# A quantised feed-forward stage: its loop written out, and its integers transposed by DMA

## What is computed

```python
def act_quant(x):
    scale = 127.0 / jnp.clip(jnp.max(jnp.abs(x), axis=-1, keepdims=True), 1e-05)
    return jnp.clip(jnp.round(x * scale), -128, 127) / scale
def bit_linear(x, w):          # w is quantised to -1, 0, 1 times a scale
    return jnp.einsum('bsd,hd->bsh', act_quant(x), weight_quant(w))
h = bit_linear(layernorm(x), w1)                  # 128 -> 512
h = depthwise_conv1d(h, conv_w, conv_b)           # three taps along the sequence
h = silu(h)
x = x + tanh(g_ffn[1]) * bit_linear(h, w2)        # 512 -> 128
```

## Time and profile before

| | |
|---|---|
| median of 3 runs | 987.94 us (987.78 to 988.53) |
| profiled execution | 991.65 us, its span 989.9 us |
| busy in the span: PE, PEld | 947.1 us (96%), 739.9 us (75%) |
| DVE, ACT, POOL | 833.3 us (84%), 748.9 us (76%), 588.4 us (59%) |
| quantised stage | from about 803 us to the end |
| DMA over the span | 21.49 MB, mean 22 GB/s |

### The profile page before, as it was taken

How to read it: one execution, slowest core, us unless ns; L and a number is a source line. 1 busy time by engine, 2 the same in 40 slices (tenths; PEclk the granted TensorE clock), 3 DMA queues, 4 the chain that set the end, 5 groups by cost and what they waited for, 6 DMA issues and landing times.

```text
span 989.9 us, 36747 instructions
## 1 busy us (share of the span) xinstructions
PE 947.1 (96%) x11854; PEld 739.9 (75%) x11854; DVE 833.3 (84%) x2349; ACT 748.9 (76%) x1709; POOL 588.4 (59%) x1232
## 2 busy tenths in 40 slices
PE   6999999999989999999899999999999899999997
PEld 4777777777779999998877677676777667777775
DVE  7888888889978888888887888888887778889886
ACT  5878787787787777766656777777777878888885
POOL 5545454544536555656885544545454378888884
PEclk9999999999999999999998999999999999999999
DMA  3501011100000000000000000000000000000001
GB/s 110 178 24 43 25 38 32 32 22 11 13 2 1 0 0 0 0 0 0 2 12 24 13 12 21 11 21 11 21 11 1 2 10 22 23 22 21 24 21 31
DMA packets 19361, 21.49 MB, mean 22 GB/s; under 512 B 3553, under 2 KB 12001, under 8 KB 19297
## 3 DMA queue, kind: packets, MB, share of 16 engines
q1 hardware_dynamic: 19296, 20.68, 6.9%
HBM read 16.48 MB, written 4.19 MB: 21 GB/s over the span
## 4 chain that ended last, share of the span: by engine, by line
PE 39%; issue 5%; POOL 4%; DVE 2%; ACT 2%; DVEq 0%; POOLq 0%; ACTq 0%
PE bank L1295 9%; PE bank L1318 7%; PE score L1372 4%; PE score L1579 2%; PE score L1581 2%; PE bank L1438 2%; PE score L1580 2%; PE score L1364 2%; PE bank L1342 2%; PE bank L1334 1%; PE bank L1330 1%; PE bank L1337 1%; ACT prob_t L599 1%; PE bank L1604 1%; POOL xdq L573 1%
## 5 line engine op out<-in xcount | busy, mean ns | idle before, releaser
L599 ACT ACTIVATE prob_t<-bank 128x512 f32<-128x512 f32 x256 | 152.8, 597 | 122.1 <-PE bank L1295 114.0
L952 DVE TENSOR_REDUCE smax<-score 128x16 f32<-128x1024 f32 x128 | 156.8, 1225 | 46.0 <-PE score L1372 30.2
L1295 PE MATMUL bank<-const,prob 128*128 128x128 f32 x1024 | 165.9, 285 | 14.1 <-ACT prob_t L599 14.1
L594 ACT ACTIVATE prob<-prob 128x512 f32<-128x512 f32 x256 | 161.2, 630 | 8.9 <-DVE prob L961 8.2
L1318 PEld LDWEIGHTS bank<-vb,prob_t 128*64 128x64 f32 x4096 | 130.4, 138 | 49.4 <-issue 42.9
L961 DVE TENSOR_TENSOR prob<-score,smax 128x512 f32<-128x512 f32 x256 | 165.0, 686 | 1.3
L1295 PEld LDWEIGHTS bank<-const,prob 128*128 128x128 f32 x1024 | 108.0, 141 | 67.6 <-issue 58.6
L1318 PE MATMUL bank<-vb,prob_t 128*64 128x18 f32 x4096 | 143.2, 213 | 0.0
L411 POOL TENSOR_SCALAR kj<-k_sb,const 128x512 f32<-128x512 f32 x124 | 85.5, 696 | 73.7 <-issue 38.5
L674 ACT ACTIVATE eb_t<-eb,gwt 128x128 f32<-128x128 f32 x256 | 81.4, 391 | 41.7 <-POOL eb_acc L452 24.7
L382 POOL TENSOR_TENSOR a_ve<-a_mv,const 128x4 f32<-128x4 f32 x32 | 6.5, 203 | 153.3 <-DVE a_mv L954 145.7
(11 more groups left out here) (162 smaller groups left out, 2334.6 us busy)
## 6 DMA issues: line engine op xcount, KB each, us to landing
ctx_t<-in_ctx SPq DMA_DIRECT2D x32, 256.0 KB, 2.7
x_all<-in_x SPq DMA_DIRECT2D x16, 256.0 KB, 2.8
out_x<-x_all SPq DMA_DIRECT2D x64, 64.0 KB, 1.5
ew<-in_ew SPq DMA_DIRECT2D x2, 512.0 KB, 5.8
f_cw<-in_f_cw SPq DMA_DIRECT2D x1, 768.0 KB, 7.9
w_t<-in_w_attn SPq DMA_DIRECT2D x2, 256.0 KB, 4.3
f_w<-in_f_w SPq DMA_DIRECT2D x2, 256.0 KB, 6.7
eb<-in_L_ffn_eb SPq DMA_DIRECT2D x1, 256.0 KB, 6.4
```

Of the source, the lines that this page charges most:

```text
L594: act.activation(v, v, ACT.Exp, scale=SCALE).then_inc(s["exp_done"], 1)
L599: act.activation(prob_t[:, 4 * half:4 * half + 4, :].rearrange("p i q -> p (i q)"), bank[PT], ACT.Copy).then_inc(s["p_copied"], 1)
L952: dve.tensor_reduce(smax[:].rearrange("p (r h) -> p r h", r=RH), sc, AX.X, ALU.max).then_inc(s["smax_done"], 1)
L1295: return pe.transpose(dst, src, ident)
```

## The change

The 64 steps of the quantised stage are written out on all five engines, so that no loop is left in it. And the integers `q2b` of a tile are transposed by a DMA that SyncE issues, straight into `q2t`. TensorE's four products L1611, ScalarE's copy L827, the unit matrix `eye16` and the semaphores `q2_tr` and `q2_copied` go. SyncE's own `ffn` issues for tile t the transpose, once `q2_int` has counted its integers and the output product of tile t-2 has freed `q2t`'s buffer, and behind it the store of tile t-2. TensorE's output products wait for the DMA of their tile; VectorE's `q2b` waits for the DMA of the tile two before, whose buffer it writes over.

```diff
-            def store(t, par, has):
-                wait(sp, "x_out", t + 1)
-                sp.dma_start(out[bass.ds(t, 1)].rearrange("o p d -> p (o d)"), x_tile(t)).then_inc(stored, 16)
-
-            run_tiles(sp, store, 0, 0)
+            def ffn(t, par, has):
+                if has(0):
+
+                    in_registers(sp, t + 1, t - 1)
+                    sp.wait_ge(s["const_in"], 16)
+                    wait(sp, "q2_int", t + 1)
+                    wait(sp, "out_mm", t - 1)
+                    sp.dma_start_transpose(q2t[:, par, :].rearrange("p (c n) -> p c n", c=FC), q2b[:, par, :])\
+                        .then_inc(q2t_in[par], 16)
+                if has(-2):
+                    wait(sp, "x_out", t - 1)
+                    sp.dma_start(out[bass.ds(t - 2, 1)].rearrange("o p d -> p (o d)"), x_tile(t - 2)).then_inc(stored, 16)
+
+            lead_in(ffn, 0, T + 1)
...
-            run_tiles(pool, ffn, 4, 2, lo=4, first=-2, body=4)
+            lead_in(ffn, -2, T + 1)
...
-                if has(-4):
-                    wait(act, "q2_tr", t - 3)
-                    wait(act, "out_mm", t - 5)
-                    act.activation(q2t[:, par, :], bank[PT], ACT.Copy).then_inc(s["q2_copied"], 1)
...
-            run_tiles(act, ffn, 5, 5, lo=6, first=2, body=4)
+            lead_in(ffn, 2, T + 4)
...
                     wait(dve, "q2_ready", t - 2)
-                    wait(dve, "q2_tr", t - 4)
+                    if has(-5):
+                        dve.wait_ge(q2t_in[o], q2t_loads(t - 5, o))
...
-            run_tiles(dve, ffn, 5, 5, lo=6, first=2, body=4)
+            lead_in(ffn, 2, T + 4)
...
                 if has(-4):
-                    wait(pe, "q2_copied", t - 3)
+                    pe.wait_ge(q2t_in[par], q2t_loads(t - 4, par))
...
-                if has(-3):
-                    wait(pe, "q2_int", t - 2)
-                    wait(pe, "q2_copied", t - 3)
-                    for c in range(FC):
-                        last = pe.matmul(bank[PT][:, c * P:(c + 1) * P], q2b[:, o, c * P:(c + 1) * P], eye16[:],
-                                         start=True, stop=True)
-                    last.then_inc(s["q2_tr"], 1)
...
-            run_tiles(pe, ffn, 5, 4, lo=6, first=2, body=4)
+            lead_in(ffn, 2, T + 3)
```

More of the change, by code:

```diff
@@ L175, in build @@
         hact = hid_b[:, 2:4, :]
-        eye16 = sb("eye16", [P, P], BF16)
         q2b = sb("q2b", [P, 2, F], BF16)
@@ L195, in build @@
             conv_mm hpre_done silu_done q2_ready
-            q2_int q2_tr q2_copied out_mm x_out""".split()
+            q2_int out_mm x_out""".split()
         s = {n: sem(n) for n in names}
@@ L199, in build @@
         ctx_ld = [sem(f"ctx_ld{i}") for i in range(2)]
+        q2t_in = [sem(f"q2t_in{i}") for i in range(2)]
         stored = sem("stored")
@@ L291, in group_loads, with q2t_loads @@
             return 2 * f + 16 - 8 * gpar
+        def q2t_loads(t, par):
+            return 8 * t + 16 - 8 * par
         def shifted(taps, par, k):
@@ L893, in _ @@
             dve.tensor_copy(ident16[:], const[:, C_ID2:C_ID2 + P]).then_inc(s["ident16_done"], 1)
-            dve.tensor_copy(eye16[:], ident).then_inc(s["ident16_done"], 1)
             dve.wait_ge(s["vb_set"], 1)
@@ L1653, in _ @@
             pe.wait_ge(s["w2t_copied"], 1)
-            pe.wait_ge(s["ident16_done"], 2)
-            run_tiles(pe, ffn, 5, 4, lo=6, first=2, body=4)
+            pe.wait_ge(s["ident16_done"], 1)
+            lead_in(ffn, 2, T + 3)
 def constants(np):
```

## The result

The changed kernel takes 980.69 us (median of 20 runs), the kernel before 989.54 us (20 runs beside it). The ratio is 0.9914, with an interval from 0.9892 to 0.9935: 8.5 us less, with bounds of 6.4 and 10.7. The forecast was 980.9 us and 7.0 us less. One run of the changed kernel, 1038.20 us at a granted clock of 0.846, is left out of the ratio.

What follows compares the result with a forecast made beforehand. Ring R, through three engines, was taken to bound the kernel, falling from 2.938 to 2.81 us a step: 7.4 + 0.4 - 0.8 = 7.0 us less, 987.94 to 980.9 us, range 977.5 to 988.5.

Steps and rivals of the forecast that it cites:

- ring R: Waits through TensorE, VectorE and GpSimd over three steps: 9.03 us before, forecast 8.43, or 2.81 a step.
- Loop ends: VectorE's loop end in ring R: writing out the loops takes 0.40 us off, 9.03 to 8.63 us.
- Products: TensorE's four products L1611 in ring R, once per turn: removing them takes off 0.20 us, 8.63 to 8.43.
- that is above ring G's 2.77, so it stands: Claim that ring R, at 2.81 us a step, still bounds the changed kernel, with 0.04 to spare.
- ring G: GpSimd alone, seven instructions a step without a wait: 2.77 us, from which the change takes nothing.
- rival 5: Ring G alone bounds, at 2.77 us a step: 9.7 us over 58 steps, 978.6 us; chance 0.62 together with the forecast.
- ScalarE's copy at zero: ScalarE's copy L827, 581 ns a step and in neither ring: removing it gains 0.
- The DMA hidden: DMA transpose in the steady steps: landing taken as 2.7 us, costs 0 while under 4.5 us.
- SyncE: Rival 2: the transpose holds SyncE, deciding from a hold of 2.5 us; at 3.0 us, +29 us; chance 0.05.
- The end: Kernel end: the last tile's DMA costs 0.8 us more, bounds -0.4 to +0.9; steps 62 and 63 give 0.4 back.
- Rival 3: VectorE and GpSimd hinder each other more, `q2b` 0.25 us longer every turn: 2.89 a step, 985.7 us; chance 0.12.

Runs made afterwards that it cites:

- early aggregation: VectorE's aggregation `ln_mv` moved ahead of the maximum over the hidden values; in the written-out kernel with the products: 982.32 us, ratio 0.9922.
- doubled transpose: Changed kernel with each tile transposed by DMA twice, first into a spare buffer, then into place: 1020.85 us in one execution.
- halves: Each part alone against the kernel before: written out with products kept, 984.13 us, ratio 0.9971; DMA transposes with four engines' loops kept, 988.87 us, ratio 0.9982.
- two kernels with early aggregation: `ln_mv` moved ahead of the maximum over the hidden values, in the written-out kernel with products (982.32 us) and in the changed kernel (979.5 us).
- looped kernel with early aggregation: Kernel before, loops and products kept, with VectorE's `ln_mv` and its wait for the statistics moved earlier: 986.67 us, ratio 0.9972.

## Why the prediction was right

**The two rings.** Right, and the lower of the two is what bounds. One turn of ring R in the changed kernel, GpSimd and VectorE timelines:

```profile
868.89 0.37 POOL L586 TENSOR_SCALAR xdq<-q,sc_i 128x128 f32<-128x128 f32 x1
...
872.05 0.69 DVE L1262 TENSOR_TENSOR hid_b<-score,f_cb 128x512 f32<-128x512 f32 x1 [0.20 <-PE score L1590]
...
872.92 0.43 DVE L1235 TENSOR_SCALAR q2b<-hid_b 128x512 bf16<-128x512 f32 x1
...
874.51 0.17 DVE L262 BATCH_NORM_AGGREGATE ln_mv<-ln_st 128x2 f32<-128x6 f32 x1
...
874.76 0.19 POOL L271 TENSOR_TENSOR ln_ve<-ln_mv,const 128x1 f32<-128x1 f32 x1
...
877.11 0.37 POOL L586 TENSOR_SCALAR xdq<-q,sc_i 128x128 f32<-128x128 f32 x1
```

The same legs of a turn in the three kernels, from the starts in the earlier trace rows and above. The sums are three steps of each kernel, whichever ring bounds; what tells the kernels apart are the legs:

| leg | before | written out | changed |
|---|---|---|---|
| `xdq` to `hpre` (TensorE) | 3.38 | 3.40 | 3.16 |
| `hpre` to `q2b` (VectorE) | 1.27 | 0.88 | 0.87 |
| `q2b` to `ln_ve` (VectorE) | 1.93 | 1.84 | 1.84 |
| `ln_ve` to `xdq` (GpSimd) | 2.45 | 2.41 | 2.35 |
| turn of three steps | 9.03 | 8.53 | 8.22 |

**Loop ends, taken at 0.40: right, a little small.** The second leg lost 0.39. The third lost 0.09 more: `q2b` took 0.48 us behind the loop end and takes 0.43 now, which is 0.05 of it. **Products, taken at 0.20: 0.24.** The fourth leg, which I held constant, is 0.10 shorter in this turn and 0.04 longer in the next (2.49, with a longer `ln_nr`). In sum I put the turn at 8.43 where it is no longer than 8.22 to 8.35 (in the changed kernel ring R is no bound, so its own length may be less; but `ln_ve` starts 0.08 to 0.09 us behind the end of `ln_mv` in all 52 steps from 813 to 955 us, as close as where it had waited, so the two rings are about level there). Three small terms, none above 0.1, decided the order of two rings that I had 0.04 us a step apart: the step "that is above ring G's 2.77, so it stands" is the one that failed. What holds is rival 5, ring G alone, at 2.757 where 2.77 was read. It was counted with the forecast, and it is worth 3 us: 58 steps gave 10.5 us and not 7.4. And ring G was not the constant that I took it for ("the change takes nothing from this"): its step without waits was 2.80 us written out with the products, 2.810 with the early aggregation too, and 2.757 in the changed kernel.

**ScalarE's copy at zero.** Nothing contradicts it: ScalarE waits 43.6 us for TensorE's L1304 in the stage, so it has room. No run took the copy away alone.

**The DMA hidden.** Right. It lands in 2.4 us (taken: 2.7), with 4.5 allowed, and nobody waits for it until the end. The estimate from the Trainium skill, "VectorE: DVE Perf Modes", The three transpose paths (four blocks of 1309 ns, 5.2 us) doesn't hold for this shape: 128x512 took 2.4 us. The same page's advice (Rules for kernel authors), to use TensorE where a destination in PSUM will do and the DMA otherwise, looks at the operation alone; here the result had to be copied on out of PSUM, and TensorE's order lay in ring R. The kernel with the DMA was the faster one: ratio 0.9914 (0.9892 to 0.9935) against 0.9971 (0.9940 to 1.0003) for the written-out kernel with the products.

**SyncE.** I had only the 338 ns of a plain store. The hold is 1.19 us for a transpose (median, 1.87 at most); 2.5 was the point from which it decides, and the doubled transpose shows that it does.

**The end, mis-sized.** I took 0.8 us for the last tile's landing and 0.4 us back from two steps. The last tile's way from `q2b` to its product is 972.32 to 975.68, 3.36 us against 1.99: 1.4 more. I had left out SyncE's order. The transpose of tile 62 holds it to 972.49, the store of tile 60 from 972.55 for 0.57 us, and only at 973.22 the last transpose is issued, 0.90 us after its integers are there. The last `q2b` had itself waited 0.72 us for the DMA of tile 61, whose buffer it takes; before it waited 0.33 us. Net, the end costs 1.1 and not 0.4.

**Rival 3** was half of the truth. VectorE's `q2b` hardly stretches (0.42 to 0.43), but GpSimd's `ln_nr` beside it does, 0.29 and 0.43 in turn for 0.19. I had looked at the wrong engine. The row of 0.68 us is the rare case: there GpSimd's `tap_lo` had started 0.01 us ahead (820.32, 0.41 us), and `q2b` ended 0.28 us behind it. As a rule `q2b` starts first: in the changed kernel all 51 `ln_nr` from 815 to 955 us start 0.03 to 0.21 us into a `q2b` and end 0.04 to 0.06 us behind its end, as if they waited for it. A GpSimd step without that would be, by an estimate, 2.757 - (0.10 + 0.24) / 2 = 2.59 us. The trace before had such rows too (`ln_nr` of up to 0.48 us), but not always in the same place.

**The total.** 10.5 - 1.1 = 9.4 us in the two profiled executions, 8.5 us by the ratio, 7.0 forecast. That 980.69 was measured where 980.9 stood is luck: the steps gave 3.1 us more than I took, the end took 0.7 us more, and the kernel before measured 989.54 us beside it where I had started from 987.94.

**Why the halves don't add up.** GpSimd's wait appears once in a body of four steps, so before, a body is one turn of ring R across the loop end and one step of GpSimd alone: (9.03 + 2.77) / 4 = 2.95, measured 2.938. The DMA alone shortens one turn in four steps by 0.24, or 0.06 a step, and gives back up to 0.2 / 4 = 0.05 in TensorE's longer gap: 0.01, measured 0.029. Written out, every turn counts, three steps each: 0.24 / 3 = 0.08, and 2.849 - 2.757 = 0.092 was measured. But the model fits that number in part by chance, since ring R doesn't bound the changed kernel. The two kernels with early aggregation divide the 0.092: relieving ring R brings 2.849 - 2.810 = 0.039 with the products still there, and the other 0.053 is GpSimd's own step, which is shorter when `q2b` falls on `ln_nr` and not on `tap_lo`. So the DMA is worth three times as much in the written-out kernel (0.092 for 0.029) for two reasons: the critical turn comes more often, and `q2b` has moved against GpSimd's instructions. That the second comes from the DMA's edit is shown; that it would come in another kernel is not. I had this pattern in the rows of before (13 waits in 50 steps) and should have used it for the half runs.

**Left open.** How the 2.881 of the looped kernel with early aggregation divides between loop ends and stretched instructions; and what part the loop ends of GpSimd and ScalarE have, which were not tried alone.

## What to carry to other kernels

Where two rings of waits lie within 2% of each other, price the lower one first: it is a floor that needs no sum, and it held here to 0.5%, while the upper one, summed over four legs, was 1 to 2.5% off. But even the step of one engine that never waits moved by 2%, from 2.757 to 2.810, with what another engine did beside it. An edit in a loop is worth its time by how often the turn that waits last comes by: once a body in a loop, once every three steps without it; so a part may show next to nothing alone, and one loop left on one engine takes most of the gain back. Moving work to a DMA queue pays while somebody else has time to wait, and at the very end of a kernel nobody has: order the last issues by who waits for them.

## What the runs showed of the hardware

- A DMA transpose of 128x512 bf16 from SBUF to SBUF: 2.4 us from issue to landing, 3.4 at most, and 1.19 us (1.87 at most) during which SyncE does nothing else. In this kernel DMA packets went from 19361 (page of before) to 54195.

```profile
DMA packets 54195, 30.09 MB, mean 31 GB/s; under 512 B 38368, under 2 KB 46816, under 8 KB 54112
```

- A plain store of 64 KB behind such a transpose holds SyncE 0.57 us for 0.34 and lands in 1.8 us for 1.5. With the products in place of the transposes it stayed at 0.34 in the written-out kernel too, so the transposes do it.
- A loop end costs the kernel 0.49 us a body on VectorE and 0.46 on TensorE where the other engines have none. TensorE's gap shows as 0.2 us with four short products ahead of it and as 0.4 without them.
- GpSimd's instructions stretch when they start during VectorE's 128x512 `q2b` (f32 to bf16): `ln_nr` from 0.19 to 0.27 to 0.45 us in the changed kernel, `tap_lo` from 0.41 to 0.59 to 0.68 in the written-out kernel with early aggregation. `ln_nr` ends 0.04 to 0.06 us behind `q2b`, `tap_lo` 0.26 to 0.28. Eight `ln_nr` of the latter kernel that start 0.01 to 0.02 us ahead of `q2b` take 0.19. What holds them was not tested.
